# A mixture-of-experts stage: tokens of batch 0 sorted by expert through indexed transfers, batch 1 summed by token with the gates on the vector engine

## What is computed

```python
x = hidden_states.reshape(-1, H)                 # H = 128
probs = jax.nn.softmax(x @ wg.T, axis=-1)        # 8 experts
topk_w, topk_idx = jax.lax.top_k(probs, 2)
topk_w = topk_w / jnp.sum(topk_w, axis=-1, keepdims=True)
expert_w = jnp.sum(jax.nn.one_hot(topk_idx, E, dtype=x.dtype) * topk_w[..., None], axis=1)
h1 = jnp.einsum('th,eih->tei', x, w1)            # i = 256
h3 = jnp.einsum('th,eih->tei', x, w3)
y = jnp.einsum('tei,ehi->teh', jax.nn.silu(h1) * h3, w2)
out = jnp.einsum('te,teh->th', expert_w, y)
```

## Time and profile before

| what | value |
|---|---|
| median of 3 runs | 278.3 us (276.68 to 278.51) |
| profiled execution, its own time | 279.73 us |
| its span (first to last instruction) | 278.0 us |
| mean granted TensorE clock | 0.978 of full |

### The profile page before, as it was taken

One profiled execution on the slowest core, in us unless ns is written; L12 is line 12 of the kernel. 1 busy time (PEld: TensorE's weight loads), 2 busy tenths in 40 slices (PEclk: granted clock), 3 DMA queues, 4 the chain that ended last, 5 costly groups with the idle time before them and its releaser, 6 DMA issues.

```text
span 278.0 us, 4261 instructions
## 1 busy us (share of the span) xinstructions
PE 256.4 (92%) x1294; PEld 158.6 (57%) x1294; DVE 189.1 (68%) x577; ACT 159.2 (57%) x298; POOL 121.4 (44%) x183
## 2 busy tenths in 40 slices
PE   7968899989998999999988989999999999999980
PEld 3345665766664755767643747457575565565630
DVE  5457878785999798466554698625989645545573
ACT  1568577776789767878686646684252423332300
POOL 9973191184332443325343420034562754554431
PEclk9968999999999999999999999999999999999995
DMA  7920000020001200000222000000000000000011
GB/s 250 343 81 1 2 0 1 2 63 15 2 0 39 112 4 4 0 0 4 75 75 75 2 1 0 2 1 0 2 0 0 1 2 0 0 0 0 2 38 38
DMA packets 5861, 8.62 MB, mean 31 GB/s; under 512 B 720, under 2 KB 3280, under 8 KB 5712
## 3 DMA queue, kind: packets, MB, share of 16 engines
q1 hardware_dynamic: 5264, 7.57, 8.6%
q10 hardware_dynamic: 576, 0.79, 0.9%
HBM read 7.83 MB, written 0.52 MB: 30 GB/s over the span
## 4 chain that ended last, share of the span: by engine, by line
PE 81%; ACT 8%; DVE 4%; issue 3%; DMA 1%; POOL 1%; POOLq 0%; DVEq 0%; ACTq 0%
PE psA L878 10%; PE psB L907 10%; PE psO L1016 10%; PE psO L930 9%; PE psB L785 4%; PE psJ L814 3%; PE psB L786 3%; PE psB L787 3%; PE psA L786 3%; PE psA L787 2%; PE psA L785 2%; ACT prob L1118 2%; PE psO L935 2%; PE psJ L891 2%; PE psJ L791 2%
## 5 line engine op out<-in xcount | busy, mean ns | idle before, releaser
L1298 DVE CUSTOM_DVE_ANT_0 junk<-psA,c 128x128 bf16<-128x128 f32 (+3 forms) x128 | 56.0, 487 | 15.0 <-PE psA L878 14.5
L756 POOL TENSOR_TENSOR gated<-silu,wbc 128x512 f32<-128x512 f32 x32 | 40.9, 1285 | 42.0 <-DVE hid L1414 21.9
L1118 ACT ACTIVATE prob<-psB 128x512 f32<-128x512 f32 (+1 forms) x88 | 47.5, 560 | 12.4 <-PE psB L907 10.5
L878 PE MATMUL psA<-kst,qa 128*128 128x512 f32 (+1 forms) x88 | 38.4, 451 | 3.3 <-ACT kst L1081 1.8
L907 PE MATMUL psB<-qb,kst 128*128 128x512 f32 (+3 forms) x128 | 38.7, 346 | 1.5 <-DVE kc L1240 0.6
L1172 ACT ACTIVATE silu<-psA 128x512 f32<-128x512 f32 x32 | 19.2, 600 | 35.5 <-PE psA L787 35.1
L1404 DVE SCALAR_TENSOR_TENSOR silu<-silu,psA 128x512 f32<-128x512 f32 x32 | 21.8, 682 | 19.7 <-ACT silu L1172 19.6
L1303 DVE TENSOR_REDUCE negm<-psA 128x3 f32<-128x462 f32 (+1 forms) x48 | 25.8, 579 | 13.0 <-PE psA L878 12.9
L1016 PE MATMUL psO<-hid,w 128*128 128x512 f32 x64 | 32.7, 593 | 0.0
L907 PEld LDWEIGHTS psB<-qb,kst 128*128 128x128 f32 x128 | 22.8, 188 | 16.4 <-issue 7.4
L741 POOL TENSOR_SCALAR_AFFINE_SELECT prob<-prob 128x256 f32<-128x256 f32 x32 | 13.0, 407 | 42.6 <-ACT prob_more L1118 42.6
(11 more groups left out here) (152 smaller groups left out, 504.5 us busy)
## 6 DMA issues: line engine op xcount, KB each, us to landing
c<-w_dram SPq DMA_DIRECT2D x8, 256.0 KB, 2.8
w<-w_dram SPq DMA_DIRECT2D x1, 1024.0 KB, 4.8
c<-c_dram SPq DMA_DIRECT2D x1, 666.0 KB, 7.8
xT<-xt_dram SPq DMA_DIRECT2D x2, 256.0 KB, 5.0
x_tok<-x_dram SPq DMA_DIRECT2D x1, 512.0 KB, 9.0
out_dram<-x_tok SPq DMA_DIRECT2D x2, 256.0 KB, 2.3
wx<-wx_dram SPq DMA_DIRECT2D x1, 384.0 KB, 7.1
c<-c_dram ACTq DMA_DIRECT2D x1, 320.0 KB, 6.4
```

The lines of the kernel that those rows point to most:

```text
L756: nc.gpsimd.tensor_tensor(gated[:, n % 2, :], silu[:, n % 2, :], wbc[:, (E * b + f // 2) % 2, :], ALU.mult).then_inc(s_sg, 1)
L878: last = nc.tensor.matmul(ps[:, c:c + heads * width].rearrange("p (n w) -> p n w", n=heads), qa[:, u % SLOTS, 128 * i:128 * i + 128], keys ...
L1118: nc.scalar.activation(dst, psB[n % SIZE["B"]][:, 0:cols], ACT.Exp, scale=SCALE).then_inc(b_done[n % SIZE["B"]], 1)
L1298: last = nc.vector.tensor_tensor_reduce(out=junk[:, p, cols], in0=psA[p][:, cols], in1=c32[:, C_MASK + S - width:C_MASK + S], scale=-1.0, ...
```

## The change

**Row 0.** Its 512 tokens x 2 experts are sorted into `NT` = 15 tiles of 128 places, each tile of one expert. `RT` (DVE, PE, DVE) counts for each token how many earlier ones chose the same expert, and makes the place of each of its two copies. `SX` on POOL writes the tokens to a buffer in memory by these places, in 8 indexed transfers of 128 rows of 512 B. `TE` works out each tile's expert and PE reads 15 numbers from it into registers. `XL` (SP) reads four tiles at a time back, `XS` transposes them and splits them into high and low. For each tile t, `R1` multiplies its 128 tokens (now the stationary operand) with w1 and w3 of its expert together, three products of 512 columns, at an address from a register; ACT takes the tanh of 256 columns, DVE makes two products of 256 columns; `R2` transposes twice, ACT copies, `R3` multiplies with w2 (two fp32 matmuls of 128 columns, address from a register), ACT copies. `YD` (SP) writes two tiles of results to memory, `YG` (POOL) gathers them back by token in 8 indexed transfers, and `YC` (DVE, 8 operations) adds both with their gates to the residual.

**Row 1.** `F1` and `F3` are as before. The product by `wbc` on POOL is gone; DVE L1611 multiplies silu and the w3 product directly. `F2` now makes tokens on partitions, expert by expert: 8 fp32 matmuls of 128 columns into one J bank, and DVE adds it to `z2` with the gate as a scalar for each partition, in 4 operations.

**Gone for both:** `WT`, `BC`, the ACT copies to `wbc`, the POOL products, `YE`, `YT`, the bf16 gate parts. **Moved:** `MP` of stage 1 from POOL to DVE. **At the start:** one transfer of 0.98 MB on SP clears the sort buffer from the zeros in slot 3 of `kst`, and the fourth unit's stack waits for it. The constants change size a little (c16 smaller by 224 KB, c32 larger by 136 KB).

The core of the diff:

```diff
-        add("MP", (u,), [("POOL", 0.55)], [("A", (u, len(fills) - 1))] + ([(("MT", (u - 2,)), 0)] if u >= 2 else []))
+        add("MP", (u,), [("POOL", 0.55) if st == 0 else ("DVE", 0.4)], [("A", (u, len(fills) - 1))] + ([(("MT", (u - 2,)), 0)] if u >= 2 else []))
...
+            add("RT", (), [("DVE", 0.55), ("PE", 0.6, 0), ("DVE", 1.7)], [("LG", (0,))])
...
+                elif kind == "XL":
+                    k, = args
+                    n = min(4, NT - 4 * k)
+                    if k == 0:
+                        sp.wait_ge(s_sx, 16 * 2 * QT)
...
+                    sp.dma_start(xs[:, k % 2, 0:D * n].rearrange("p (t d) -> p t d", d=D),
+                                 xs_d[512 * k:512 * k + 128 * n, :].rearrange("(t p) d -> p t d", p=128)).then_inc(s_xl[k % 2], 16)
...
-                    nc.gpsimd.tensor_tensor(gated[:, n % 2, :], silu[:, n % 2, :], wbc[:, (E * b + f // 2) % 2, :],
-                                            ALU.mult).then_inc(s_sg, 1)
+                elif kind == "SX":
...
+                    nc.gpsimd.indirect_dma_start(
+                        out=xs_d[:, :], out_offset=bass.IndirectOffsetOnAxis(ap=place_u[:, QT * k + i:QT * k + i + 1], axis=0),
+                        in_=x_tok[:, 0, i, :], in_offset=None).then_inc(s_sx, 16)
+                elif kind == "YG":
...
+                    nc.gpsimd.indirect_dma_start(
+                        out=back[:, k, i, :], out_offset=None, in_=ys_d[:, :],
+                        in_offset=bass.IndirectOffsetOnAxis(ap=place_u[:, QT * k + i:QT * k + i + 1], axis=0)).then_inc(s_yg, 16)
...
+                elif kind == "F2":
...
+                    for i in range(QT):
+                        for f in (2 * e, 2 * e + 1):
+                            last = nc.tensor.matmul(ps[:, 128 * i:128 * i + 128], hid[:, f % 4, 128 * i:128 * i + 128],
+                                                    w2[:, 128 * f:128 * f + 128], start=f == 2 * e, stop=f == 2 * e + 1)
...
+                elif kind == "TE":
+                    pe.wait_ge(s_te, 1)
+                    for t in range(NT):
+                        expert_at.append(pe.value_load(tile_u[0:1, t:t + 1], min_val=0, max_val=I * (E - 1)))
...
+                elif kind == "R1":
...
+                    w = [wp[:, :, p, bass.ds(expert_at[t], I)] for p in range(PAIR)]
+                    nc.tensor.matmul(ps, xr_high[:, t % 8, :], w[0], start=True, stop=False)
+                    nc.tensor.matmul(ps, xr_low[:, t % 8, :], w[0], start=False, stop=False)
+                    nc.tensor.matmul(ps, xr_high[:, t % 8, :], w[1], start=False, stop=True).then_inc(s_a, 1)
...
+                    for n in range(2):
+                        at = I * (t % 2) + 128 * n
+                        last = nc.tensor.matmul(ps[:, 0:128], hT[:, at:at + 128], w2[:, bass.ds(expert_at[t] + 128 * n, 128)],
+                                                start=n == 0, stop=n == 1)
...
+                    dve.wait_ge(s_rth, t + 1)
+                    link(nc.vector.scalar_tensor_tensor(out=th[:, t % 2, :], in0=th[:, t % 2, :], scalar=1.0, in1=ps[:, 0:I],
+                                                        op0=ALU.add, op1=ALU.mult))
...
+                    nc.vector.tensor_tensor(hs[:, t % 2, :], th[:, t % 2, :], ps[:, I:2 * I], ALU.mult).then_inc(a_done[a % SIZE["A"]], 1)
+                elif kind == "YC":
+                    dve.wait_ge(s_yg, 16 * 2 * QT)
```

More of the change, by code:

```diff
@@ L23 @@
 WC = 4
+NT = S * 2 // 128 + E - 1
 PARTS = 3
+PAIR = 2
 ROWS = 3 * HD
@@ new lines, in tasks @@
+    add("TE", (), [("DVE", 0.5), ("PE", 1.5)], [("RT", ())])
+    for k in range(-(-NT // 4)):
+        add("XL", (k,), [("SP", 0.6)], [("SX", (1, QT - 1)), ("CQ2", (1,))] + ([(("XS", (k - 2,)), 0)] if k >= 2 else []), after=2.2)
+        add("XS", (k,), [("PE", 0.44), ("ACT", 0.5), ("DVE", 0.6)], [("XL", (k,))],
+            [(1, (("R1", (4 * k - 5,)), 0))] if k >= 2 else [])
+    for t in range(NT):
+        late = [(1, (("R1", (t - 2,)), 2)), (2, (("R2", (t - 2,)), 0))] if t >= 2 else []
+        add("R1", (t,), [("PE", 0.72), ("ACT", 0.32), ("DVE", 0.8)],
+            [("XS", (t // 4,)), ("TE", ()), ("WS", (2 * WC - 1,)), (("SQ", (1, 1, NG - 1)), 0)], late)
+        add("R2", (t,), [("PE", 0.24), ("ACT", 0.32)], [("R1", (t,))], [(1, (("R3", (t - 2,)), 0))] if t >= 2 else [])
+        add("R3", (t,), [("PE", 0.46), ("ACT", 0.22)], [("R2", (t,)), ("W2", ())], [(1, ("YD", (t // 2 - 2,)))] if t >= 4 else [])
+        if t % 2 or t == NT - 1:
+            add("YD", (t // 2,), [("SP", 0.6)], [("R3", (t,))], after=2.2)
@@ new lines, in tasks @@
+    for n in range(2 * QT):
+        add("YG", divmod(n, QT), [("POOL", SEND)], [("YD", ((NT - 1) // 2,)), last_pv(NU - 1)], after=2.2)
+    add("YC", (), [("DVE", 2.0)], [("YG", (1, QT - 1)), ("GATE", (0,)), ("LNX", (1, 1))])
+    for f in range(FT):
+        add("F1", (f,), [("PE", 0.69), ("ACT", 0.49), ("DVE", 0.6)], [("XT", (1, 1)), ("WS", (WC - 1,))],
+            [(1, ("F3", (f - 2,)))] if f >= 2 else [])
+        add("F3", (f,), [("PE", 0.69), ("DVE", 0.6)], [(("F1", (f,)), 0), ("WS", (2 * WC - 1,))],
+            [(1, ("F1", (f,)))] + ([(1, (("F2", (f // 2 - 2,)), 0))] if f >= 4 else []))
+        if f % 2:
+            add("F2", (f // 2,), [("PE", 1.76), ("DVE", 0.95)], [("F3", (f,)), ("W2", ())], [(1, ("GATE", (1,)))])
@@ L301, in tasks @@
     for b in range(B):
-        add("YE", (b,), [("ACT", 0.49)], [("F2", (b, FT - 1)), (("OP", (1, 1)), 0)] + ([(("YT", (0,)), 0)] if b else []))
-        add("YT", (b,), [("PE", 0.44), ("DVE", 0.75)], [("YE", (b,))], [(1, ("LNX", (1, 1) if b == 0 else (2, 0)))])
-        add("LN", (2, b), [("DVE", 1.2), ("POOL", 1.3)], [("YT", (b,))])
+        add("LN", (2, b), [("DVE", 1.2), ("POOL", 1.3)], [("F2", (E - 1,)) if b else ("YC", ())])
         add("LNX", (2, b), [("DVE", 1.05)], [("LN", (2, b))])
@@ L319, in schedule @@
             key = what if isinstance(what[0], tuple) else last(what)
-            extra = table[key[0]][2] if key == last(key[0]) else 0.0
+            extra = 0.0 if isinstance(what[0], tuple) else table[key[0]][2]
             before[item, n].append((key, LATENCY[table[key[0]][0][key[1]][0]] + extra))
@@ L484, in layer_kernel @@
         ot_sb = sb("ot_sb", [128, S])
-        junk = sb("junk", [128, SIZE["A"], S], BF16)
+        junk = shared("junk", [128, SIZE["A"], S], BF16)
+        choice = sb("choice", [128, 2, QT, E])
+        chosen = sb("chosen", [128, QT + 1, E], BF16)
+        over = sb("over", [128, E, E * QT])
+        first_tile = sb("first_tile", [128, E])
+        place = sb("place", [128, QT, E])
+        place_f = sb("place_f", [128, 2 * QT])
+        place_u = sb("place_u", [128, 2 * QT], U32)
+        before_t = sb("before_t", [1, 16, E - 1])
+        tile_f = sb("tile_f", [1, 16])
+        tile_u = sb("tile_u", [1, 16], U32)
+        sb("unused", [128, 232])
+        xs = rest
+        back = prob[:, 0, 0:2 * S].rearrange("p (k i d) -> p k i d", k=2, i=QT)
         z = sb("z", [128, QT, D])
@@ new lines, in _ @@
+                    if f >= 4:
+                        job_filled(dve, ("F2", (f // 2 - 2,)))
+                    nc.vector.tensor_tensor(hid[:, f % 4, :], psB[h % SIZE["B"]][:, :], silu[:, f % 2, :], ALU.mult).then_inc(b_done[h % SIZE["B"]], 1)
+                elif kind == "F2":
+                    e, = args
+                    ps = bank(JOB[item])
+                    if e == 0:
+                        dve.wait_ge(s_x, 4)
+                    for i in range(QT):
+                        ins = nc.vector.scalar_tensor_tensor(out=z2[:, i, :], in0=ps[:, 128 * i:128 * i + 128], scalar=gw[:, 0, i, e:e + 1],
+                                                             in1=x_tok[:, 1, i, :] if e == 0 else z2[:, i, :], op0=ALU.mult, op1=ALU.add)
+                    free(JOB[item], ins)
+                    job_free(dve, JOB[item])
```

417 lines of the change are left out of this document (259 added, 158 removed), and 4 rows, old and new, of the table RINGS.

## The result

| | before | after |
|---|---|---|
| median | 278.3 us (276.68 to 278.51, 4 runs) | 284.67 us (283.01 to 285.29, 4 runs) |
| profiled execution | 279.73, span 278.0 | 284.7, span 282.9 |
| ratio | | 1.0233, 95% interval 1.0175 to 1.0291 |

The change makes the kernel 2.3% slower, and the time lies outside the forecast's own range of 260 to 274.

What follows compares the result with a forecast made beforehand. PE was taken as the bound, busy 256.4 of 278.0 us. Gone 45.9 us, added 35.1, net -10.8: 268.9 from the profiled 279.73, or 267.5 by the median, own range 260 to 274.

Steps and rivals of the forecast that it cites:

- The register reads: Before the sorted stage, PE reads 15 numbers into registers: 2.5 us taken, bounds 1.6 to 3.3.
- rival B: PE's queue held by registers: 6.6 us of register operations, slow reads 1.5 beyond the wait; 275.6 by the median, chance 0.12.
- the sum: Whole kernel: 45.9 us of PE-path time gone, 35.1 added, net -10.8 us.
- signs of being wrong: Next profile: SX over 2 us each, halved clock, long DVE wait before YC, reads over 0.5 us, experts above 5 us apart.
- If the register reads take longer, this wait takes them up: PE's wait for sorted tokens, 4.3 us (5.0 with the split), lies behind the reads and would absorb longer ones.
- rival A: Slow indexed transfers, s = 2.35: longer waits and 3 us of lost clock; 284.7 by the median, chance 0.18.
- lost cover in general: Units before the sorted stage that now have nothing between their exponentials: 1.5 us added to PE's path.
- Close, but no bound: Row 1's experts: DVE has at most 3.9 us of work in an expert of 4.60, so it does not limit.
- s: POOL's time to issue one indexed transfer: 1.28 us taken, bounds 0.43 and 2.35.
- the 2.0 taken: Sorted stage: PE's waits for DVE through the three A banks, 2.0 us added, bounds 0 and 6.
- the large unknown: The wait for the sorted tokens, through eight indexed transfers: 5.0 us added, 0 or 13.6 at the bounds of s.
- the small one: PE's fifteen register reads before the sorted stage: 2.5 us added.

Runs made afterwards that it cites:

- run 6, r1: The changed kernel with its fifteen register reads made without the bounds check behind each: 280.74 us, ratio 1.0084 to the kernel before.
- run 2, e2: The changed kernel with one register read in place of fifteen, its value used by all tiles: 270.56 us, ratio 0.9734 to the kernel before.
- e1_const: The changed kernel with fixed expert numbers in place of the fifteen register reads: 270.25 us, ratio 0.9717 to the kernel before.
- run 15, c1: The changed kernel with constants for the reads and the planner told 0.6 us per indexed transfer, giving another order: 274.21 us, ratio 0.9871 to before.
- run 9: The changed kernel without the eight gathers of row 0's expert outputs and DVE's wait for them: 282.37 us, ratio 1.0153 to the kernel before.
- d1_dense: Against the changed kernel: no sorting, reads or indexed transfers, row 1's new way used for both rows: 270.32 us, ratio 0.9722 to the kernel before.
- a1_again: The changed kernel once more, unedited, on another chip: 285.22 us, ratio 1.0265 to the kernel before.
- e3: The changed kernel with its fifteen register reads spread, one before each of the next fifteen PE items: 278.72 us, ratio 1.0027 to the kernel before.
- r2: The changed kernel with one read instruction that fills all fifteen registers: 278.15 us, ratio 1.0002 to the kernel before.
- p1: The changed kernel with two reads of packed numbers in place of fifteen, packed by DVE, unpacked by PE: 276.54 us, ratio 0.9941 to before.
- r3: The changed kernel with one read of fifteen registers and the planner told 0.6 us per indexed transfer, giving another order: 276.29 us, ratio 0.9962 to before.
- p2: The changed kernel with two packed reads and the planner told 0.6 us per indexed transfer, giving another order: 278.10 us, ratio 1.0013 to before.

## Why the prediction was wrong

**The register reads: the step that failed, in its price.** The prediction took 2.5 us for fifteen, with bounds of 1.6 to 3.3 (its own 0.2 us each would make 3.0), from the shortest pass of PE and the smallest DVE operation. Neither row is of that kind, and neither bounds it. A read took 0.67 us, 10.05 in all. The Trainium skill gives a floor of about 600 ns for one such load (DMA: Bandwidth & Descriptors, section Latency and other measured facts). The prediction quoted it in rival B and set it aside in the sum; an estimate by it is 9 us, near the 10.05 measured. But the trace does not bear out the floor for the load itself: its record is 0.30 us, and without the two instructions behind it the loads follow each other after 0.41 us (run 6). Rival B was right in naming slow reads, and wrong in their price beyond the wait (1.5 us) and in the 6.6 us for register operations (run 2). Of the signs of being wrong that the prediction listed, this one came: reads over 0.5 us each.

**"If the register reads take longer, this wait takes them up": the overlap that failed.** There was no wait to take them up. The sum found PE's arrival by taking away the work that goes: 187.0 with reads of 2.5 us, so 184.5 with none, and tokens at 191.3. The kernel with constants has no reads and arrived at 189.85, 5.3 us later than that, just when the tokens were there. What the sum left out: the reads begin only when their numbers are written, at 177.1, and so does what stands behind them, 12.0 us of PE's work up to the sorted tokens (177.82 to 189.85 in e1_const). That alone brings PE to the tokens when they arrive, and what the reads take is added in full. PE goes on at 187.44 in place of 177.82, 9.6 us later, and then needs 13.3 us in place of 12.0, with the clock at half until 191.6. So the reads cost 10.9 us on the way (200.78 - 189.85).

**The clock.** The sum had it full until the sorted stage, and rival A had 3 us for a wait that never came. The new order has PE busy 8.00 of 10 us in 150 to 160 and 7.07 in 160 to 170 (the kernel before 9.04 and 9.25), and the clock was at half from 164.3 to 174.5. Expected was 1.5 us for lost cover in general. No run shows that this first stretch cost time, and two speak against it: the kernel with constants has 6.8 us at half clock there in place of 10.2, and its numbers are written at 177.3, not earlier than the 177.1 of the kernel after; and the higher clock of run 15 brought its tokens no sooner. The second stretch is a consequence of the reads and is counted with them above.

**The stand: not in any step.** 2.3 to 2.9 us, by run 9.

**"Close, but no bound" for DVE.** Right up to the stand, where DVE has 11.59 of 20 us (230 to 250), and wrong behind it, where it also has row 0's sum (L1590, twice 1.14) and norm to do: 19.47 of 20. From the sorted tokens to the end I forecast 77.6 us; the kernel with constants took 80.1 (269.96 - 189.85) and the kernel after 83.9. Of the 6.3 us too many the stand and what it pushes out are 3.8. The other 2.5 the kernel with constants has too. Its PE waits 0.40 and 1.86 us ahead of the last two second products, for which the sum had nothing; that these are most of the 2.5 is argued, not shown.

**What held.** Experts of 4.56 us (4.60), s = 1.26 (1.28), places at 175.0 (175.5), the router's end at 170.6 (170.9), XT at 164.7 (165.5), the tokens ready at about 189.4 (191.3), the clearing transfer hidden, register arithmetic free. PE's wait ahead of R3 of a sorted tile was 2.8 us in three pieces (1.17, 0.48, 1.13) for the 2.0 taken. So the large unknown was priced well, and the small one wrongly.

**Against the whole.** 268.9 - 1.4 (without reads PE starts on the sorted tokens at 189.85, not 191.3) + 10.9 (the reads, with the clock behind them) + 6.3 (the end) = 284.7. Rival A's number was hit by other causes, and its price s = 2.35 is refuted. That the change still had a fast half shows in d1_dense, 14.9 us under a1_again.

**Still open.** What holds DVE and ACT up in the stand. They stand together, PE and POOL go on, and in the program of the kernel after it takes more than four gathers; but e1, e2 and e3 issue the same eight at the same place of the DVE program, beside the same products, and show none. The kernel after, r1, r2 and p1, which show it, differ from those only in PE's instructions at and around the reads, and p1 in two small DVE operations. In the other order it is the same: r3 and p2 have DVE idle for 3.72 and 3.68 us ahead of a gate whose product is there, c1 has not. One candidate can be put aside: the profile shows the fetch of a block of instructions (queue q8) some 2.2 us behind the first gather in the kernel after, but in e3_spread, which has no stand, too. No run here tells which resource it is.

## What to carry to other kernels

An operation with no row in the trace has no bound from rows of another kind: where a page gives a figure for it, let that figure into the range. Before a wait is said to swallow it, ask two things: when can the operation itself begin, and how much work stands between it and the wait? Here both were fixed (numbers at 177.1, 12.0 us of work), and they left no cover. Data in registers is best packed or loaded by one instruction (2.2 us for fifteen in place of 10.1). Before a computation is made sparse, run its dense form with the same clean-ups: here the gates on DVE (with `MP` moved there) brought all of the 8 us, and sorting, which removed 9 us of PE's work, gave them back in waits.

## What the runs showed of the hardware

- A read of an SBUF word into a PE register took a record of 0.30 us (0.49 for the first). With the two instructions that check its value it holds PE's queue for 0.67 us, without them for 0.41; fifteen by one instruction made a stretch of 2.21 us, with a record of 1.89. Meanwhile the matmuls behind it wait, and DVE and ACT run dry.
- An indexed transfer of 128 rows of 512 bytes holds POOL for 0.94 to 0.96 us (1.24 and 1.11 for the first of a group) and follows the one before after 1.25 to 1.27, in both directions (DRAM written by index, DRAM read by index).
- PE's granted clock was at half for 10.2 us behind a stretch in which PE was busy for 2.06 of 5 us, and it fell once more while PE was idle. With spread reads PE counted as busy and its clock was near half (0.53, 0.50 and 0.61 in three stretches of 5 us).
- In the kernel after DVE and ACT stood for about 3 us beside the fifth to eighth of eight gathers; with four gathers or none they did not. Four kernels with all eight (e1, e2, e3 and c1) did not show it either, and these runs did not find the condition.
